# Self attention's products moved from behind both score steps of a batch to between them, half a batch later

## The reference

```python
q = (x @ Wq.T).reshape(Bv, Tv, H, D).transpose(0, 2, 1, 3)
k = (x @ Wk.T).reshape(Bv, Tv, H, D).transpose(0, 2, 1, 3)
v = (x @ Wv.T).reshape(Bv, Tv, H, D).transpose(0, 2, 1, 3)
scores = jnp.einsum('bhqd,bhkd->bhqk', q, k) / scale
bias = jnp.where(causal_mask[None, :, :], -jnp.inf, bias)
scores = scores + bias[None]
attn = jax.nn.softmax(scores, axis=-1)
out = jnp.einsum('bhqk,bhkd->bhqd', attn, v)
```

## Time and profile before

| | us |
|---|---|
| median of 3 runs | 2228.96 |
| the 3 runs | 2227.3, 2228.96, 2253.64 |
| the profiled execution, its time | 2229.1 |
| its span, first to last instruction | 2227.2 |

### The profile page before, as it was taken

The page is one execution under the profiler, slowest core; times in us unless marked ns, Lnnn a source line. Parts: engine busy times, 40 slices in busy tenths (PEclk is TensorE's granted clock), DMA queues, the critical chain, the costliest instruction groups (busy, mean ns, idle before and its releaser), DMA issues.

```text
span 2227.2 us, 32080 instructions
## 1 busy us (share of the span) xinstructions
PE 1968.5 (88%) x11994; PEld 1077.4 (48%) x11994; DVE 1246.3 (56%) x2495; ACT 878.4 (39%) x1762; POOL 1026.8 (46%) x856
## 2 busy tenths in 40 slices
PE   6888998889998999999999999999899899889662
PEld 3544444444444555545555555555555555545331
DVE  3667666776513655636545545645544654653668
ACT  2235556666644242123333343343343343334331
POOL 1000000000002583237766667766776776769774
PEclk9759879999968899679999999999999999999875
DMA  4322202240010000000000000000000000000001
GB/s 91 38 32 30 29 2 31 31 92 2 11 38 29 8 1 8 1 1 10 1 1 11 1 1 11 1 1 11 1 1 3 1 1 4 1 28 1 1 19 38
DMA packets 27746, 34.63 MB, mean 16 GB/s; under 512 B 3986, under 2 KB 25811, under 8 KB 25939
## 3 DMA queue, kind: packets, MB, share of 16 engines
q1 hardware_dynamic: 27592, 32.59, 8.1%
HBM read 14.99 MB, written 4.19 MB: 9 GB/s over the span
## 4 chain that ended last, share of the span: by engine, by line
PE 75%; DVE 10%; issue 6%; ACT 4%; POOL 2%; DMA 1%; SPq 1%; POOLq 0%; DVEq 0%; ACTq 0%
PE psum L854 17%; PE psum L839 13%; PE psum L827 7%; PE psum L747 7%; DVE maxima L1104 7%; PE psum L661 5%; PE psum L722 5%; PE psum L695 4%; PE psum L843 4%; ACT weights_room L940 4%; PE psum L877 3%; PE psum L865 2%; PE psum L815 2%; PE psum L759 2%; PE psum L731 1%
## 5 line engine op out<-in xcount | busy, mean ns | idle before, releaser
L1104 DVE TENSOR_REDUCE maxima<-psum 128x1 f32<-128x400 f32 (+5 forms) x1664 | 881.5, 582 | 446.4 <-PE psum L827 278.1
L1345 POOL TENSOR_TENSOR parts_room<-parts_room,weights_room 128x512 f32<-128x512 f32 (+1 forms) x596 | 746.6, 1286 | 329.1 <-ACT weights_room L998 329.1
L998 ACT ACTIVATE weights_room<-psum 128x512 f32<-128x512 f32 (+1 forms) x694 | 369.3, 598 | 611.2 <-PE psum L843 607.8
L940 ACT ACTIVATE weights_room<-psum 128x512 f32<-128x512 f32 (+3 forms) x640 | 297.9, 535 | 247.3 <-PE psum L722 132.6
L1307 POOL TENSOR_SCALAR rstd<-meanvar 128x2 f32<-128x2 f32 (+1 forms) x24 | 6.7, 277 | 701.0 <-DVE meanvar L1054 701.0
L839 PE MATMUL psum<-stack_room,k_hi 64*128 64x512 f32 (+1 forms) x1664 | 303.5, 411 | 9.5 <-ACT weights_room L998 7.9
L827 PE MATMUL psum<-k_hi,stack_room 64*128 64x400 f32 (+1 forms) x1024 | 261.8, 419 | 33.0 <-DVE maxima L1104 30.7
L827 PEld LDWEIGHTS psum<-k_hi,stack_room 64*128 64x128 f32 x1024 | 152.5, 196 | 208.4 <-issue 118.6
L722 PE MATMUL psum<-stack_room,stack_room 51*128 51x512 f32 (+3 forms) x640 | 202.6, 454 | 40.8 <-ACT weights_room L940 39.0
L839 PEld LDWEIGHTS psum<-stack_room,k_hi 64*128 64x128 f32 (+1 forms) x1664 | 168.8, 186 | 58.2 <-issue 28.2
L843 PE MATMUL psum<-shifts,parts_room 64*128 64x512 f32 (+1 forms) x832 | 191.3, 399 | 0.0
(11 more groups left out here) (119 smaller groups left out, 1798.6 us busy)
## 6 DMA issues: line engine op xcount, KB each, us to landing
stack_room<-parts_room SPq DMA_DIRECT2D x96, 128.0 KB
x_block<-x_dram SPq DMA_DIRECT2D x8, 512.0 KB, 4.7
x_middle<-x_block SPq DMA_DIRECT2D x4, 512.0 KB, 3.1
x_block<-x_middle SPq DMA_DIRECT2D x4, 512.0 KB, 5.5
out_dram<-x_block SPq DMA_DIRECT2D x8, 256.0 KB, 2.1
parts_room<-ctx_dram SPq DMA_DIRECT2D x1, 1536.0 KB
stack_room<-shift_rows SPq DMA_DIRECT2D x64, 2.0 KB
parts_room<-wq_dram SPq DMA_DIRECT2D x8, 128.0 KB, 2.3
```

The source lines that it names most:

```text
L940: engine.activation(w_self[s % NW][:, m, 0:n], self_scores[(HP * s + m) % SELF_SCORES][:, 0:n], ACT.Exp, scale=SELF_SCALE).then_inc(exp_do ...
L998: engine.activation(weights[u % NP_WEIGHTS][:kw, :], pair_scores[u % NSCORES][:kw, :], ACT.Exp, scale=CROSS_SCALE).then_inc(pair_exp, 1)
L1104: engine.tensor_reduce(maxima[:, p % 2, i // TB, n, i % TB, ch:ch + 1], bank_of(use + n)[:, 0:real - k0], AX.X, ALU.max) \
L1345: engine.tensor_tensor(sum_[:kw, m, :], old[:kw, :], new, ALU.add).then_inc(weights_added, 1)
```

## The change

The two edits below change only the list. Each batch is now S, V, S. The pair of steps is handed over to `pending` when its second step is placed, and `values(1)` leaves one whole batch waiting, so the V between the two steps of batch k is that of batch k - 2. During the final drain `values()` leaves none waiting, as before. The rest of the diff is blank lines; every line of the engines' programs has a number one higher than before (L723 is L722 of before, and so on).

```diff
-    def values(self):
+    def values(self, behind=0):
         for _ in range(2):
             self.pass_step()
-        if self.pending:
+        if len(self.pending) > 2 * behind:
             p, b, j, s = self.pending[0]
             self.put("values", p, b, j, s)
             if j + 2 == TB * b + TB:
                 self.put("finish", p, b)
                 self.after(FOLD_LAG, lambda: self.fold(p, b))
-        self.pending = self.pending[2:]
+            self.pending = self.pending[2:]
@@ sweep2 @@
             self.batch.append((p, b, j, self.step))
             self.step += 1
-
-        def values():
-            self.values()
-            self.pending, self.batch = self.batch, []
+            if len(self.batch) == 2:
+                self.pending, self.batch = self.pending + self.batch, []
 
         steps = []
         for b in range(NB):
             for j0 in range(0, TB * b + TB, 2):
                 work = [min(TB, TB * b + TB - j) / TB for j in (j0, j0 + 1)]
-                steps += [(w, lambda b=b, j=j: scores(b, j), b) for w, j in zip(work, (j0, j0 + 1))]
-                steps.append((2 * work[0], values, b))
+
+                steps.append((work[0], lambda b=b, j=j0: scores(b, j), b))
+                steps.append((2 * work[0], lambda: self.values(1), b))
+                steps.append((work[1], lambda b=b, j=j0 + 1: scores(b, j), b))
```

## The result

| | before | after |
|---|---|---|
| median, us | 2226.82 (20 runs, 2196.62 to 2253.64) | 2244.18 (20 runs, 2223.44 to 2391.83) |
| ratio | | 1.0089 [1.0053, 1.0124] |
| profiled execution, its time and span | 2229.1, 2227.2 | 2228.72, 2226.8 |

The change costs 0.9%, some 20 us, where 5 us were forecast: a small loss as predicted, well inside 2%, but larger than the sum that gave it. The median of 2244.18 us lies in the inner range of the forecast (2230 to 2245 us), at its very edge. The ratios here leave disturbed executions out, so they are not quite the quotients of the medians.

What follows compares the result with a forecast made beforehand. PE's own work was taken as the bound (busy 88% of 2227.2 us). Losses of 6 us in six pairs and 0.5 in pair 0, less 1 us in pair 7, made +5 on 2229.1: 2234 us, range 2211 to 2260.

Steps and rivals of the forecast that it cites:

- The cycle is relabelled: Long runs of full tiles: S S V and S V S are one cycle; a pair-7 batch stays 2.60 us.
- The lag is free: V's extra half batch of lag: gains nothing and costs 0, since the needed V stands immediately ahead on PE.
- The count of pairs of steps: Pairs 1 to 5: of 20 pairs of steps, 10 stood bare (without a chunk) before and 8 do now.
- The new shapes: Diagonal steps of a block, bare: (384,256) waits some 0.40 us and (128,512) some 0.1 us.
- The banks at block 2's opening: Chunks and `rows` there wait for DVE to free banks: about 0.3, 0.7 and 0.2 us, 1.2 in all.
- The end of the sweep: Only one V now stands between the last chunk and `rows`, so `rows` waits 0.65 us, before 0.27.
- 1.0 us lost, in six pairs 6 us: Pairs 1 to 6: PE's waits come to 7.8 us a pair against 6.8 before.
- woven the same, 0.5 us: Pair 0, whose second half is woven like the later pairs: 0.5 us lost.
- the banks bind harder: Rival: bank waits 2.5 times as long, chunks bunching where a short V stands; +21 us, 2250 us; chance 0.11.
- 1 us gained: Pair 7: diagonals pair at 0.45 + 0.40 + 0.1 instead of 0.45 + 0.35 + 0.45, 0.3 us a block.
- the clock comes on top of it: Clock luck outside the sum: pairs 1 and 2 lost 18 us; another two at pair 2's loss, 23 us.
- The rival had named the direction: Rival: clustered waits keep pairs 1 to 6 at pair 2's pace, 76.2 instead of 64.7 us; 2285 us; chance 0.05.

Runs made afterwards that it cites:

- the hidden `rows` wait: The changed kernel with the last `rows` stage of pairs 2 to 6 put beside a chunk of the next pair: 2256.48 us (before 2222.95 beside it).

## Why the prediction was right, and where its sum was short

**The cycle is relabelled: right.** There is no cover by V: score waits in pair 3 are 5.4 us before and after. A pair-7 batch was to stay 2.60 us and is 2.67 (the starts 679.73 - 677.06):

```profile
677.06 0.73 PE L723 MATMUL psum<-stack_room,stack_room 51*128 51x512 f32 x3
678.31 0.50 PE L723 MATMUL psum<-stack_room,stack_room 51*128 51x512 f32 x1 [0.51 <-ACT weights_room L941]
...
679.73 0.73 PE L723 MATMUL psum<-stack_room,stack_room 51*128 51x512 f32 x3
...
683.74 0.38 PE L723 MATMUL psum<-stack_room,stack_room 51*128 51x256 f32 x1 [0.47 <-ACT weights_room L941]
...
687.76 1.08 PE L760 MATMUL psum<-fold,o_raw 128*128 128x34 f32 x8 [0.72 <-ACT o_raw L951]
```

The bare wait is 0.51 us and not 0.45, a small size error that repeats in most bare pairs (four of the five full ones in pair 3); the last fold's 0.72 us is unchanged, as said.

**The lag is free: right**, with its condition tested: the same lag with V behind the second step costs 4.6%. Half the lag costs next to nothing at full clock either.

**The count of pairs of steps: right for pairs 1 to 5.** In pair 3 ten stood bare before and eight do now.

**The new shapes: right.** (384,256) waits 0.47 us for 0.40 forecast, (128,512) 0.14 us for 0.1.

**The banks at block 2's opening: right in place and sum.** Forecast 0.3, 0.7 and 0.2 us:

```profile
356.06 0.27 PE L712 MATMUL psum<-ident,shift 128*8 128x128 f32 x1 [0.30 <-DVE maxima L1105]
356.94 0.50 PE L696 MATMUL psum<-stack_room,stack_room 51*128 51x512 f32 x2 [0.61 <-DVE maxima L1105]
...
359.80 0.50 PE L723 MATMUL psum<-stack_room,stack_room 51*128 51x512 f32 x1 [0.15 <-ACT weights_room L941]
```

0.30 and 0.61, and the third bank wait did not come. The page books the 0.30 on `rows` (L712), so L696's total stayed at 1.1 us and did not go towards 2. The wait behind the `finish` copy is 0.57 us in block 1, but 0.15 us here, each for 0.5 forecast, and that between steps 0.3 and 1.0 is absent for 0.25; in their place most bare pairs cost 0.06 us more each, and the sum of the score waits came out at the forecast 5.4 to 5.5.

**The end of the sweep: right.**

```profile
395.15 0.27 PE L712 MATMUL psum<-ident,shift 128*8 128x128 f32 x1 [0.65 <-DVE shift L1118]
```

0.65 us, as worked out, but by two errors that cancel. The last chunk starts at 392.58 us, so `rows` could go 2.57 us behind it and not 2.05; and PE needs 0.86 us, not 0.35, until the V starts. The sum for the pair at full clock is 7.5 us of idle time for 7.8 forecast (7.1 and 7.3 in the two with dips); pairs 1 to 6 together have +5.9 for +6. This total owes something to pair 6, which alone lost 2.3 us, all ahead of scores (3.8 to 6.1 us; the first row of after, the second of before):

```profile
L723 PE MATMUL psum<-stack_room,stack_room 51*128 51x512 f32 (+3 forms) x80 | 24.4, 431 | 6.1 <-ACT weights_room L941 5.8
```

```profile
L722 PE MATMUL psum<-stack_room,stack_room 51*128 51x512 f32 (+3 forms) x80 | 23.7, 424 | 3.8 <-ACT weights_room L940 3.5
```

The steps of pairs 1 to 5 were counted and pair 6 taken to be like them. It has other side work, with other places for it: bare pairs of steps went from 5 to 12 there, and not from 10 to 8. Its length says more than its idle time: 71.4 us less the 1.4 us that one dip costs (pair 4 against pair 3) is 70.0, 3.9 us more than before's 66.1, and the distances between the heads of a step rose by 3.7 us. So a term of "1.0 us lost, in six pairs 6 us" came out right as a sum while its parts did not: 0.6 us in each of five pairs and 3.9 us in the sixth.

**The step that failed first: pair 0, "woven the same, 0.5 us".** Measured +4.1 us. Pair 0 has 138 chunk records beside its scores and not 82, and DVE is 77.3 us busy in 105 us. PE is short of banks there by 7.8 us already before. The walk of bank waits was made for block 2 of pair 3 and never for pair 0, where chunks that stand together wait for DVE. The kernel with the new order in pair 0 alone bears it out (+3.4 us at equal clock; 18.2 us of idle time in pair 0 as in after, 14.1 before). It is the places of the chunks that count and not S V S as such: with a chunk between nearly all pairs of steps in the old order, pair 0 waits 14.7 us ahead of chunks too. The rival "the banks bind harder" (+21 us) had nearly the measured size, but in pair 3 chunks wait 1.1 us as before, and only in pair 0 do they wait longer.

**Pair 7: "1 us gained"** did not show. Its idle time rose by 0.5 us, but parts of the pair are at half clock, and over the profiles with the old order it runs from 8.4 to 9.6 us, against 9.3 here. The shapes pair as forecast, and the bare wait of 0.51 instead of 0.45 us in each full batch takes their gain back.

**The clock: "the clock comes on top of it", at zero.** This is the larger miss: 8 to 9 us, 0.005 of mean clock. The rival had named the direction (waits that cluster could lose the full clock) but priced it only at half clock throughout. What the profile shows is short dips. A full V takes 1.94 us instead of 1.06:

```profile
444.73 1.08 PE L760 MATMUL psum<-fold,o_raw 128*128 128x34 f32 x8
445.74 1.94 PE L748 MATMUL psum<-weights_room,v_self 128*32 128x512 f32 x8
```

Told by the durations of full V, all slow stretches of the profile of after but two begin with the first V of block 1, 2 or 3, as here; in pairs 4, 5 and 6 there are four that before did not have. One more begins at the eleventh step's V of block 3 in pair 0, behind the wait ahead of `rows`: in all five profiles whose pair 0 has the stages of after's (the later fold aside), in none with the old order, and not in the changed order with the chunk beside the second step. The Trainium skill, "TensorE: Matmul & The Clock Gate", section "A second HAM failure mode: psum-queue depth-cycling", has the clock go back and forth from short idles of PE between groups of matmuls that are frequent enough. These dips agree with it in kind, but it does not say which idles do it, and pair 3 has 14 of 0.14 to 0.57 us ahead of scores at full clock. Kernels with the new order and its full lag in pair 0 have mean clocks of 0.902 to 0.906, and before, before with the later fold, and the new order in pairs 1 to 6 have 0.911 to 0.914. But the kernel with a chunk between all pairs in the old order has 0.905 too, so pair 0's order is not the whole of it, and neither the later fold nor the hidden `rows` wait brought the changed kernel's clock back, though the later fold went with 0.918 for 0.905 in that other kernel. The cause of the 0.005 stays open; for this order the fold's place and the wait at the sweep's end were tested and do not explain it.

## What to carry to other kernels

Write a new order of a cycle down for two periods and compare it with the old one rotated: if they match, the edit can only act at the seams (block openings, sweep ends, the first and last pairs and every one with other side work), and each seam has to be walked through by itself, the most starved one first. A longer lag is free only while the instruction that frees a ring's buffer stands ahead of the one that needs it. And price a wait between two matmuls that share the array by the start-to-start distance, not by the idle column.

## What the runs showed of the hardware that was not expected

- Half clock also comes in short dips that follow the matmuls closely. The V that starts at 445.74 us takes 1.94 us, and the granted clock is 0.94 from 444 to 446 us, 0.50 from 446 to 448 and 1.00 again from 450 us on. The V at 493.7, 513.9 and 585.4 us have dips of the granted clock beside them in the same way. One such dip cost 1.4 us (pair 4 against pair 3 of after).
- A mean granted clock lower by 0.001 goes with 1.6 to 1.8 us of span here, and the runs of one kernel spread by 0.01 and more. Two single executions of equal length (2228.72 and 2229.1 us) hid a loss of 20 us.
- A step whose second head comes late costs more than its wait: with chunks between the steps, the distance between the heads fell by 3.2 us a pair and the idle time ahead of scores by 2.0 us. In pair 6 of after the distance rose by 3.7 us and the idle time by 2.3 us.
